# An attention and mixture-of-experts block on one core: transposed probabilities copied ahead of exponentials, row maxima ahead of query evictions

## What is computed

```python
h = _layernorm(x) * (1 + ca) + sa
q, k, v = jnp.einsum('bsx,xAnh->Abnsh', h, w); q = q + q_bias
a = (q @ k^T) * h ** (-0.5) + relative_causal(pos_scores)     # pos_scores from q and sinusoids
a = jax.nn.softmax(jnp.where(mask, a, NEG_INF), axis=-1)
o = jnp.einsum('bnqk,bnkh->bqnh', a, v)
x = x + ga * (o @ out_kernel + out_bias)
h = _layernorm(x) * (1 + cb) + sb
x = x + gb * moe(h)      # 16 experts, top 1, 256 places each
```

## Time and profile before

| | |
|---|---|
| median of 3 runs | 927.01 us |
| profiled execution, device time | 925.67 us |
| span of its trace | 923.7 us |
| PE, PEld busy | 874.1 us (95%), 677.9 us (73%) |
| DVE, ACT, POOL busy | 698.0 us (76%), 655.2 us (71%), 586.0 us (63%) |
| chain of work that ended last | PE 82%, DVE 5%, issue 5%, ACT 3%, POOL 2%, DMA 1% |

### The profile page before, as it was taken

How to read it: one execution, slowest core, us unless ns; L and a number is a source line. 1 busy time by engine, 2 the same in 40 slices (tenths; PEclk the granted TensorE clock), 3 DMA queues, 4 the chain that set the end, 5 groups by cost and what they waited for, 6 DMA issues and landing times.

```text
span 923.7 us, 18012 instructions
## 1 busy us (share of the span) xinstructions
PE 874.1 (95%) x5515; PEld 677.9 (73%) x5515; DVE 698.0 (76%) x2115; ACT 655.2 (71%) x1843; POOL 586.0 (63%) x917
## 2 busy tenths in 40 slices
PE   7789999999999999999999999999999999998994
PEld 6667777777767777777777776777777777766994
DVE  4878778787878788777778787878877778753784
ACT  3688777777778777777777777777787777651551
POOL 3566666667667765677666766776567666553354
PEclk9999999999999999999999999999999999999998
DMA  7332222112100101111101110010101110106661
GB/s 288 92 92 58 91 83 53 46 50 66 44 24 24 55 18 41 24 41 38 35 24 31 41 44 24 24 40 18 40 24 35 31 36 23 32 8 214 215 216 40
DMA packets 36512, 56.01 MB, mean 61 GB/s; under 512 B 7446, under 2 KB 21511, under 8 KB 36160
## 3 DMA queue, kind: packets, MB, share of 16 engines
q1 hardware_dynamic: 32624, 46.16, 17.3%
q0 software_dynamic: 3072, 5.94, 1.8%
q10 hardware_dynamic: 720, 2.75, 0.8%
HBM read 23.96 MB, written 16.82 MB: 44 GB/s over the span
## 4 chain that ended last, share of the span: by engine, by line
PE 82%; DVE 5%; issue 5%; ACT 3%; POOL 2%; DMA 1%; SPq 0%; POOLq 0%; DVEq 0%
PE bank L839 22%; PE bank L869 16%; PE bank L849 14%; PE bank L801 13%; PE bank L876 5%; PE bank L824 5%; PE bank L836 3%; POOL out L506 2%; PE bank L1015 2%; DVE xh L1249 1%; DMA kx<-in_ktab 1%; ACT prob L612 1%; PE bank L1062 1%; PE bank L897 1%; PE bank L1051 1%
## 5 line engine op out<-in xcount | busy, mean ns | idle before, releaser
L612 ACT ACTIVATE prob<-srow,nmax 128x512 f32<-128x512 f32 (+3 forms) x512 | 287.1, 562 | 178.3 <-DVE nmax L1171 176.1
L1171 DVE CUSTOM_DVE_ANT_0 srow<-bank,consts 128x512 f32<-128x512 f32 (+3 forms) x512 | 244.4, 483 | 79.8 <-issue 46.1
L454 POOL TENSOR_SCALAR prob<-prob,rsum 128x128 f32<-128x128 f32 (+3 forms) x512 | 264.9, 537 | 59.0 <-DVE rsum L1183 55.3
L849 PE MATMUL bank<-consts,prob 128*128 128x128 f32 x1280 | 204.6, 275 | 0.4 <-POOL prob L454 0.2
L849 PEld LDWEIGHTS bank<-consts,prob 128*128 128x128 f32 x1280 | 153.8, 140 | 30.9 <-ACT pt L621 9.8
L869 PE MATMUL bank<-pt,v 128*64 128x512 f32 (+3 forms) x1024 | 152.0, 438 | 15.4 <-issue 14.7
L839 PE MATMUL bank<-khi,qhi 128*128 128x512 f32 (+2 forms) x384 | 152.8, 398 | 1.7 <-DVE klo L1210 1.7
L445 POOL CAST qhi<-qx 128x384 fp32r<-128x384 f32 x128 | 65.9, 515 | 137.1 <-DVE qx L1195 124.7
L621 ACT ACTIVATE pt<-bank 128x384 f32<-128x384 f32 x318 | 151.5, 494 | 1.1 <-PE bank L849 1.0
L869 PEld LDWEIGHTS bank<-pt,v 128*64 128x64 f32 x1024 | 74.5, 136 | 95.0 <-issue 79.0
L447 POOL TENSOR_TENSOR qlo<-qx,qhi 128x384 fp32r<-128x384 f32 x128 | 131.5, 1027 | 10.7
(11 more groups left out here) (193 smaller groups left out, 1483.3 us busy)
## 6 DMA issues: line engine op xcount, KB each, us to landing
qx<-g SPq DMA_DIRECT2D x252, 64.0 KB, 2.0
xbuf<-fill SPq DMA_DIRECT2D x16, 385.0 KB, 4.1
x<-xbuf SPq DMA_DIRECT2D x16, 385.0 KB
raw<-in_w SPq DMA_DIRECT2D x16, 256.0 KB, 3.0
prob<-in_w SPq DMA_DIRECT2D x16, 256.0 KB, 3.0
out<-row SPq DMA_DIRECT2D x8, 256.0 KB, 2.6
x<-in_x SPq DMA_DIRECT2D x1, 1792.0 KB, 14.7
modb<-mod_rows SPq DMA_DIRECT2D x8, 192.0 KB, 3.6
```

Source lines behind the costliest of these rows:

```text
L454: end = gp.tensor_scalar(part, part, rsum[:, par, 4 * h + q:4 * h + q + 1], 1.0, ALU.mult, ALU.mult)
L612: act.activation(prob[:, par, h, QOFF[q]:QOFF[q] + P * (q + 1)], srow[:, k % 4, 0:P * (q + 1)], ACT.Exp, bias=nmax[:, par, k:k + 1], scale ...
L849: last = pe.transpose(out[:, n * P:(n + 1) * P], prob[:, par, h, QOFF[q] + k * P:QOFF[q] + (k + 1) * P], ident)
L1171: dve.tensor_tensor_reduce(out=srow[:, k % 4, 0:w], in0=scb[k % 2][:, 0:w], in1=mask[:, S - w:S], scale=-1.0, scalar=BIG, op0=ALU.add, op1 ...
```

## The change

Only the order of instructions changes; none is added or taken away.

- ACT: the copies of transposed groups 2, 3 and 4 stand ahead of the exponential of the same k, where they stood behind it. The copies of groups 1 and 5 stay where they were. The first key eviction (`evac_k(j + 1, 0)`) moves from behind exponential 5 to behind exponential 6.
- DVE: at k = 3 and 4 the row maximum stands ahead of the query eviction. `xhat2` moves from k = 2 and 3 to k = 1 and 2 of a = 3.
- PE: the key product moves from k = 5 to k = 6, behind scores 6. `turn_x` moves from k = 4 to k = 3 of a = 2.

```diff
@@ ScalarE, step @@
                 for k in range(8):
-                    if before and k == 5:
-                        evac_pt(j - 1, 5)
+                    if before and 1 <= k < 6:
+                        evac_pt(j - 1, k)
                     exps(j, par, k)
-                    if before and k == 0:
-                        evac_pt(j - 1, 1)
...
-                    if before and 2 <= k < 5:
-                        evac_pt(j - 1, k)
...
-                    if after and k == 5:
+                    if after and k == 6:
                         evac_k(j + 1, 0)
@@ TensorE, step @@
-                    if (a, k) == (2, 4) and not last:
+                    if (a, k) == (2, 3) and not last:
                         pe.wait_ge(s["ve"], j + 4)
                         turn_x(b + 1)
...
-                    if k == 5 and after:
+                    if k == 6 and after:
@@ VectorE, after_attention and step @@
-                if (a, k) in ((3, 2), (3, 3)):
-                    xhat2(b, range(2 * k - 4, 2 * k - 2))
+                if (a, k) in ((3, 1), (3, 2)):
+                    xhat2(b, range(2 * k - 2, 2 * k))
...
                 for k in range(8):
+                    scores(j, par, k)
                     if k in (3, 4) and after:
                         evac_q(j + 1, (a + 1) % PAIRS, k - 3)
-                    scores(j, par, k)
```

## The result

The changed kernel is **slower by 0.65%**: 935.48 us (median of 14 runs, 932.59 to 975.13) against 929.40 us for the kernel before in the same comparison (14 runs). The ratio is 1.0065, with a 95% interval of 1.0048 to 1.0083, so 4.5 to 7.7 us. Forecast was 917 us. The sign is wrong, and the time lies outside the range. Of the 18.5 us between forecast and median, 2.4 are the kernel before itself, whose median was 927.01 us when the forecast was made. The execution of 975.13 us ran at a mean granted clock of 0.85, for 0.98 to 0.99 in the others, and the ratio leaves it out.

A forecast was written before the change was run, and what follows sets the result against it. The bound was whichever wait ended last in each of eight step kinds, in the plain step the last transposed copy. Terms summed to -1.34 us a batch, about -10 us over 7.5 batches: 917.0 us, range 908 to 926.

The forecast's parts named there:

- plain step: The step a = 7, replayed in trace times: sum starts at 420.34 instead of 420.60, -0.27 us.
- New waits of the key product for `qx`: On PE in most steps: key product waits for the later query eviction; bounds nothing to 0.5 us in three kinds of step.
- The step `a = 0`: Two norm statistics between the query evictions on DVE now push row maximum 4 and the second eviction: +0.47 us.
- The key chain, a = 3 and 5: `evac_k` behind exponential 6 feeds `kx`, `klo` and the next first scores: -1.37 us at a = 3, 0 at a = 5.
- cover of 0.2 us: In the plain step `klo` stays at 421.76 and ends 0.2 us before PE's earlier end: "covered, barely".
- The second eviction, all steps but a = 4: On DVE, 0.62 us behind row maximum 4's start, overlap 0.07: ends 1.1 us later in the plain step, at 419.28.
- The end of the plain step, a = 7: Last score tile starts at 420.12, PE is free and the sum starts at 420.34: -0.27 us.
- a = 1: DVE works without a gap until `klo`; idle time ahead of row maximum 3 and small losses shift it past PE: +0.26 us.
- collision rival: At a = 1 `xhat1` meets a POOL division and takes 1.07 us more, in seven steps: 924.5 us, chance 0.06.
- slower rival: Each 0.1 us the second query eviction is later costs 0.1 us in six kinds of step: 939.5 us, chance 0.06.
- half-gain rival: Key chain or key-product wait 0.1 us longer in most steps, 0.7 us a batch: 922 us, chance 0.25.
- My bounds: Row maximum 3's start: 2 us in all; new key-product wait: -4 to +7 us; an `xhat2` half: up to 5 us.

The follow-up runs named there:

- run 1: The kernel before with only ScalarE's copies 2, 3 and 4 moved ahead of the exponential of the same number: 915.4 us, ratio 0.987.
- run 4: The kernel before with only `xhat2` moved one tile earlier, to k = 1 and 2 of a = 3: 919.4 us, ratio 0.992.
- run 6: The kernel before with ScalarE's copies ahead of the exponentials, `xhat2` one tile earlier and `turn_x` at k = 3 of a = 2: 903.5 us, ratio 0.974.
- run 10: The changed kernel with the first key eviction on ScalarE behind exponential 5 again: 924.9 us, ratio 0.996.
- run 11: The changed kernel with VectorE's first reciprocal moved between row maximum 4 and the second query eviction: 937.3 us, ratio 1.010.
- run 7: The changed kernel with the query evictions ahead of the row maxima again at k = 3 and 4: 921.6 us, ratio 0.992.
- run 12: run 6 with `normed` at k = 3 of a = 2 and `residual2` behind `klo` and the second reciprocal of a = 1: 900.15 us, ratio 0.970.

## Why the prediction was wrong, point by point

**What held.** The replay of the plain step up to row maximum 4: row maxima 3 and 4 start 5.56 and 6.68 us into it, for 5.55 and 6.71. The copies are no longer last (run 1: -12 us). `xhat2` at 0.60 us a half, in the changed kernel and in run 4. `turn_x` for nothing (run 6). New waits of the key product for `qx` and, at a = 3 and 5, of the first scores for `klo`: both are there. The step `a = 0` at +0.47 (measured +0.61), a = 4 at 0.

**What failed: the sizes in the replay of what stands behind row maximum 4.** The waits were the right ones, but every chain behind the second eviction was taken as a little too short, in all kinds of step but a = 4. Forecast and measurement differ by 2.1 us a batch, over 7.5 batches 16 us: more than the gain of 10 us that was expected. By steps the differences are 0.14, 0.37, 0.28, 0.41, -0.03, 0.41, 0.21 and 0.30 us. The terms:

- *The key chain, a = 3 and 5* (forecast -1.37 and 0). The second eviction's end at 8.09 us of the plain step, as replayed, and the reciprocal and row maximum 5 behind it with an overlap of 0.07 us each, give 8.09 + 0.18 + 0.56 - 2 x 0.07 = 8.69 us for the end of row maximum 5. It was done at 8.97, 0.28 us later, and exponential 5, exponential 6, `khi`, `kx` and `klo` stand in a row behind it. Run 10 prices the whole chain at 0.57 and 0.67 us, 1.2 us a batch. The prediction had counted 0.28 of it at a = 3 (11.94 for 11.66) and 0.5 at a = 5, so some 0.46 of the 0.82 us missed at these two steps are the chain's. The rest is PE's own pace, 11.77 and 11.76 us in run 10 where the prediction had 11.66 and 11.5. I had seen this chain, and had even called its cover of 0.2 us in the plain step bare, but gave it the benefit of a replay without gaps. The prediction also has the second eviction of a = 3 end 1.4 us earlier. That is about what the move of `xhat2` does alone (1.26 us, run 4); the row maximum ahead of it takes most of this back, and in the changed kernel it ends 0.39 us earlier (8.18 us into the step for 8.57).
- *The second eviction, all steps but a = 4.* I let it overlap with row maximum 4 by 0.07 us, and the reciprocal and row maximum 5 behind it likewise. They don't overlap (run 11). That is 0.09 us at the key product (8.23 for 8.14), and 0.3 us at row maximum 5. At a = 0, 2 and 6 the forecast missed by 0.14, 0.28 and 0.21 us; how these divide was not measured. The row that shows it was before me: in the earlier trace rows the second eviction runs from 417.40 for 0.76 us, and row maximum 4 starts at 418.19, 0.03 us *behind* its end, where I used the overlap of the other neighbours.
- *The end of the plain step, a = 7* (forecast -0.27, measured +0.03). I counted 0.22 us from the start of the last score tile to the sum. Where nothing else is late, PE takes 0.31 us (run 7: 8.93 to 9.24 us in its plain step), and in the changed kernel 0.42, since the weights of that tile wait for row maximum 5: its row takes 0.49 us where the earlier trace rows have 0.39. So of the 0.50 us of stall that the prediction saw ahead of the sum only some 0.4 was to be had: run 1 won 0.37.
- *a = 1* (forecast +0.26, measured +0.63). 0.1 us are the hand-overs. The rest is `xhat1`: its two pairs took 0.76 and 0.97 us in the kernel before, and take 1.13 and 0.86 us here, 0.26 us more. That is the collision rival in a small form, which I had given 1.07 us or nothing. The kernel before, and then the changed one:

```profile
344.09 0.76 DVE L1116 TENSOR_SCALAR xn<-x,mom,rstd 128x128 f32<-128x128 f32 x2
...
345.12 0.97 DVE L1116 TENSOR_SCALAR xn<-x,mom,rstd 128x128 f32<-128x128 f32 x2
```

```profile
354.73 1.13 DVE L1112 TENSOR_SCALAR xn<-x,mom,rstd 128x128 f32<-128x128 f32 x2
...
356.11 0.86 DVE L1112 TENSOR_SCALAR xn<-x,mom,rstd 128x128 f32<-128x128 f32 x2
```

**Where the method failed.** The slower rival had this mechanism, the eviction behind one more row maximum in every step, and its price rule of 0.1 us in six kinds of step. Its chance was 0.06 against 0.55 for the replay. But the eviction itself was only 0.09 us later than worked out in the plain step (8.18 for 8.09), which by that rule is 4 of the 16 us. The rest lies in what stands behind it and in `xhat1`. The half-gain rival had the place, the key chain or the new wait 0.1 us longer, but priced it at 0.7 us a batch where 2.1 were missed, 0.26 us a step on average. The terms came out of one replay with the same optimistic hand-over, so their errors have the same sign and add up over 60 steps. My bounds treated the start of row maximum 3 and the new wait as independent, a few microseconds each. A replay that ends in "covered, barely" or "-0.27" in most steps had no more accuracy than the hand-overs in it, about 0.1 us for each of three or four in a row.

And the parts were never costed one by one. The prediction gives a sum for each step. Had it asked for each part what it does by itself, the row maxima would have stood there with the eviction 1.1 us later for copies that ScalarE's own order already frees: in run 1 copy 5 ends at 8.94 us of the plain step, and PE itself would start the sum at 8.63 + 0.31 = 8.94. The sum started at 9.05, so an earlier row maximum 4 has 0.1 us at most left to win there.

## What to carry to other kernels

When a change reorders three engines at once, price each part alone and against the others, by the chain that each one ends: here two parts gained 23 us (25 with `turn_x`), and one swapped pair of instructions in each step took all of it back and more. An instruction for which another engine waits (the second query eviction) should not go behind one that is only urgent on its own engine. Before believing a gain of some tenths per step, take the hand-over between *these* neighbours from a row, with the tiles' partitions in view, and see what the sum is if each is 0.1 us longer.

## What the runs showed of the hardware

- **VectorE's neighbours overlapped on the same partitions and not across them.** Row maximum, reciprocal and row maximum on all partitions follow each other with an overlap of 0.08 us. An eviction that reads partitions 64 to 127 and writes from 0 started 0.03 us behind the end of its predecessor, and the next instruction to read that memory did so too: 0.11 us for each hand-over, three in the changed kernel (428.87 to 428.91, 429.67 to 429.69, 429.87 to 429.90), two in run 11, and two in the kernel before (417.37 to 417.40, 418.16 to 418.19). The Trainium skill has a model of this (VectorE: DVE Perf Modes, "Two Vector instructions with no wait between them"): an instruction is held until all earlier ones have finished when it starts in another group of 32 partitions than the last read or write of the same memory. By that rule, run 11 should have had two holds for three, and the trace agrees, with the reciprocal at 7.32 and row maximum 5 at 8.31 us.
- **A DVE instruction that meets a POOL instruction can be kept until that ends.** 1.03 us for an instruction of 0.33 us that started 0.06 us behind a POOL subtraction of 1.00 us and ended 0.09 behind it (run 11). By the rule that the prediction cited (the Trainium skill, SBUF — State Buffer, "SBUF: two separate sides") the one that starts first on the shared port pair keeps it for its whole instruction, and this row agrees. The slow pair of the earlier trace rows doesn't by the profile's starts: its second instruction starts at 367.53, 0.09 us ahead of POOL's subtraction, and still takes 1.17 us and ends 0.08 us behind it. Nor does each meeting cost: the `place` instruction that took 0.58 us at a = 5 of run 11 took 0.25 in the changed kernel, within one of POOL's divisions (405.99, in a row of four from 405.19 to 407.27). What the prediction lacked was where such a meeting falls: 0.67 us of shift on POOL, set off by one reciprocal on DVE, decides on 0.4 us of step a = 1.
- **The releaser that is named can be a bystander.** PE's idle time at the end of a = 1, 3 and 5 was put down to POOL, whose last instruction belonged to another head. Moving one instruction on ScalarE removed it at a = 3 and 5 (run 10). At a = 1 it stayed, since DVE's own work ends last there (`klo` at 358.37, the scores at 358.47). In run 6 0.26 us of it are left, and run 12 removed them by moving `residual2`.
